# A patch-layout scratch image, the split of a new image one period later, and the blend in the middle of VectorE's period

## The reference, cut to what matters

```
def step(u, _):
    ux, uy, uxx, uxy, uyy = _derivs(u)          # 3x3 and 5x5 stencils, clipped to +-10
    g2 = ux * ux + uy * uy
    denK = jnp.maximum(1.0 + g2, EPS)
    K = jnp.clip((uxx * uyy - uxy * uxy) / (denK * denK + EPS), -5.0, 5.0)
    denH = jnp.sqrt(1.0 + g2 + EPS)
    H = ((1.0 + uy * uy) * uxx - 2.0 * ux * uy * uxy + (1.0 + ux * ux) * uyy) / (2.0 * denH ** 3 + EPS)
    H = jnp.clip(H, -5.0, 5.0)
    u = u + DT * jnp.clip(alpha * K + beta * H, -1.0, 1.0)
    return jnp.pad(u[:, :, 1:-1, 1:-1], ((0, 0), (0, 0), (1, 1), (1, 1)), mode='edge')
mixed = 0.7 * u_after_10_steps + 0.3 * x        # layer 0
out = conv(relu(conv(mixed, w1) + b1), w2) + b2 + mixed   # layer 1
```

## Time and profile before

| | us |
|---|---|
| median of 3 runs (40586.49 to 40609.12) | 40605.43 |
| the profiled execution, its own time | 40599.69 |
| its span in the trace | 40597.9 |
| PE busy | 34779.5 (86%) |
| DVE busy | 34223.0 (84%) |
| ACT busy | 33168.8 (82%) |
| POOL busy | 20444.4 (50%) |

### The profile page before, as it was taken

One profiled execution on the slowest core, in us unless ns is written; L12 is line 12 of the kernel. 1 busy time (PEld: TensorE's weight loads), 2 busy tenths in 40 slices (PEclk: granted clock), 3 DMA queues, 4 the chain that ended last, 5 costly groups with the idle time before them and its releaser, 6 DMA issues. The chain is left out here.

```text
span 40597.9 us, 445411 instructions
## 1 busy us (share of the span) xinstructions
PE 34779.5 (86%) x120896; PEld 22578.0 (56%) x120896; DVE 34223.0 (84%) x31730; ACT 33168.8 (82%) x33722; POOL 20444.4 (50%) x7685
## 2 busy tenths in 40 slices
PE   5888888888888888888888888888888888888999
PEld 3555555555555555555555555555555555554444
DVE  8999999999999999999999999999999999994111
ACT  5888889888888889888888889888888889885333
POOL 3555555555555555555555555555555555551000
PEclk9999999999999999999999999999999999999999
DMA  7555556555555555555555556555555556554333
GB/s 181 79 78 79 79 75 76 77 79 79 79 79 79 79 74 76 77 79 79 78 78 79 79 74 77 77 79 78 79 79 79 78 76 76 77 78 88 99 99 97
DMA packets 2728323, 3335.51 MB, mean 82 GB/s; under 512 B 2236356, under 2 KB 2236484, under 8 KB 2422212
## 3 DMA queue, kind: packets, MB, share of 16 engines
q1 hardware_dynamic: 2727364, 3324.78, 56.8%
HBM read 626.33 MB, written 301.47 MB: 23 GB/s over the span
## 5 line engine op out<-in xcount | busy, mean ns | idle before, releaser
L645 PE MATMUL tame_slot<-tame_split,tame_M 128*128 128x512 f32 x51200 | 15359.2, 422 | 5684.4 <-DVE tame_ux L516 3252.1
L645 PEld LDWEIGHTS tame_slot<-tame_split,tame_M 128*128 128x128 f32 x51200 | 9234.4, 192 | 11664.9 <-DVE tame_cross L516 3060.2
L645 PE MATMUL tame_slot<-tame_halo,tame_M 112*128 112x512 f32 x51200 | 14449.7, 404 | 0.0
L357 POOL TENSOR_TENSOR tame_split<-tame_U,tame_split 128x1024 fp32r<-128x1024 f32 x2560 | 6230.8, 2434 | 12957.1 <-ACT tame_split L392 12957.1
L645 PEld LDWEIGHTS tame_slot<-tame_halo,tame_M 112*128 112x128 f32 x51200 | 9855.4, 192 | 2544.4
L369 POOL TENSOR_TENSOR tame_ux<-tame_ux,tame_cross 128x1024 f32<-128x1024 f32 x2560 | 8063.4, 3150 | 436.3 <-POOL tame_ux L363 436.3
L363 POOL TENSOR_TENSOR tame_ux<-tame_ux,tame_uy 128x1024 f32<-128x1024 f32 x2560 | 6151.2, 2403 | 2695.9 <-DVE tame_uy L516 2695.9
L655 PE MATMUL tame_slot<-tame_uxy,tame_unit 128*128 128x512 f32 x10240 | 4962.0, 607 | 7.2 <-DVE tame_slot L539 7.2
L432 ACT ACTIVATE tame_slope<-tame_slope 128x2048 f32<-128x2048 f32 x2560 | 4894.9, 1912 | 0.0
L427 ACT ACTIVATE tame_slope<-tame_slope 128x1024 f32<-128x1024 f32 x2560 | 2717.5, 1062 | 2153.1 <-issue 2151.1
L558 DVE TENSOR_TENSOR tame_uyy<-tame_slot,tame_slope 128x1024 f32<-128x1024 f32 x2560 | 3135.7, 1225 | 1201.1 <-PE tame_slot L655 1189.8
(11 more groups left out here) (58 smaller groups left out, 36779.3 us busy)
## 6 DMA issues: line engine op xcount, KB each, us to landing
tame_halo<-tame_split SPq DMA_DIRECT2D x2560, 520.0 KB
tame_halo<-tame_split SPq DMA_DIRECT2D x2560, 260.0 KB
tame_halo<-tame_split SPq DMA_DIRECT2D x5120, 65.0 KB
xin<-mixed SPq DMA_DIRECT2D x672, 319.0 KB, 4.3
tame_U<-in_x SPq DMA_DIRECT2D x256, 512.0 KB, 3.7
tame_stage<-in_x SPq DMA_DIRECT2D x128, 1024.0 KB, 8.4
mixed<-tame_stage SPq DMA_DIRECT2D x1024, 128.0 KB, 2.5
out<-res SPq DMA_DIRECT2D x672, 192.0 KB
```

The costliest lines, as they stand in the source:

```text
L357: nc.gpsimd.tensor_tensor(split_rows(c, 1), half_rows(c), split_rows(c, 0).bitcast(F32), ALU.subtract).then_inc(lo_ready, 2)
L645: last = nc.tensor.matmul(ps[name][:, b * BANK:(b + 1) * BANK], M[0:lanes, matrix, :], rows(c, part)[:, b * y:(b + 1) * y, :], start=(n < ...
```

## The change

In layer 0 it does five things.

- `mixed` keeps the patch layout: one partition's 8 KB stay together, and a store is one DMA instead of ten.
- Even and odd columns swap their halves of a patch row (`place`); the partitions that exchange and edge copies touch form the same pattern as before.
- `high` and `low` of a chunk come one period later (k-4 instead of k-3). `scale` moves from the end of ACT's period to behind `copy_ux` of the next one, and `blend` from the start of DVE's period to behind `multiply_first`.
- SP's period is in another order: first `edge_columns` and `edge_rows` of chunk k-2 together, then stage load and half load, then the whole `exchange`, then the store.
- All eight copies of an exchange are issued in one go.

In layer 1 the two side strips of an `xin` row are no longer loaded. DVE makes them (`wrap`, two copies of 63 columns), a row is loaded in pieces of 256 B, and each product is one matmul of 512 columns and four of 256. The loop over 86 units is unrolled.

```
 def place(c):
-    return c // 2 + c % 2 * (PC // 2)
+    return c // 2 + (1 - c % 2) * (PC // 2)
...
             def store(r, i):
-                for to, col, x0, n in ([(PX + k * PX, k, 0, PX) for k in range(PC)]
-                                       + [(1, PC - 1, 0, PX - 1), (PX + PC * PX, 0, 1, PX - 1)]):
-                    sp.dma_start(rows[:, :, to:to + n],
-                                 tile[place(col):P:PC, :, x0:x0 + n]).then_inc(stored[i % 2], 16)
+                image = mixed[bass.ds(r // (C // SLOTS), 1), :, bass.ds(r % (C // SLOTS) * SLOTS + i, 1), :, :]
+                sp.dma_start(image.rearrange("b r o g c -> (b r o) g c"), stage[i % 2][:, :]).then_inc(stored[i % 2], 16)
 
             def period(t, k, kind, r):
+                c = k - 2
+                if exists(kind, c):
+                    edge_columns(t, c)
+                    edge_rows(t, c)
...
-                filling = k % 2 == 0 and kind != "tail" and not (kind == "last" and k == CHUNKS - 2)
-                image, j = (k + 2) % CHUNKS // 2, (k + 2) % 4 // 2
-                if filling:
+                if k % 2 == 0 and kind != "tail" and not (kind == "last" and k == CHUNKS - 2):
                     sp.wait_ge(lo_ready, split_done(t, k - 5))
                     sp.sem_inc(split_whole, 1)
                     if not (kind == "first" and k == 0):
                         sp.wait_ge(product[LAST_FIELD], done(t, k - 1))
-                    exchange(image, j, 0)
-                c = k - 2
-                if exists(kind, c):
-                    edge_columns(t, c)
-                if filling:
-                    exchange(image, j, 1)
-                if exists(kind, c):
-                    edge_rows(t, c)
+                    exchange((k + 2) % CHUNKS // 2, (k + 2) % 4 // 2)
...
-                if exists(kind, k - 3) and goes_on(kind, k - 3):
-                    low(t, k - 3)
+                if exists(kind, k - 4) and goes_on(kind, k - 4):
+                    low(t, k - 4)
...
+                if exists(kind, k - 3) and ends(kind, k - 3):
+                    scale(r, k - 3)
...
-                if exists(kind, k - 3) and goes_on(kind, k - 3):
-                    next_high(t, k - 3, kind, r)
+                if exists(kind, k - 4) and goes_on(kind, k - 4):
+                    next_high(t, k - 4, kind, r)
...
-                if exists(kind, k - 2) and ends(kind, k - 2):
-                    scale(r, k - 2)
...
             def period(t, k, kind, r):
-                if exists(kind, k - 3) and ends(kind, k - 3):
-                    blend(t, k - 3, r)
...
                     multiply_first(t, k)
+                if exists(kind, k - 3) and ends(kind, k - 3):
+                    blend(t, k - 3, r)
...
+            def load(b, u):
+                signal = x_top_in if u == 0 else x_bottom_in if u == UNITS - 1 else x_in[(u - 1) % BUFS]
+                for p0, y, n in rows_of(u):
+                    rows = mixed[bass.ds(b, 1), y % PR:y % PR + n, :, :, y // PR * PX:(y // PR + 1) * PX]
+                    sp.dma_start(source(u)[p0:p0 + n * C, PX:PX + W],
+                                 rows.rearrange("b r c g x -> (b r c) g x")).then_inc(signal, 16)
...
+                nc.vector.tensor_copy(t[:, 1:PX], t[:, HALF:HALF + PX - 1])
+                nc.vector.tensor_copy(t[:, PX + W:PX + W + PX - 1], t[:, PX + HALF + 1:PX + HALF + PX]).then_inc(
+                    x_wrapped, 1)
...
             def product(out_ps, weights, cols, src):
-                for dx in range(K):
-                    last = nc.tensor.matmul(out_ps, weights[:, dx, 0:cols], src[:, dx * PX:dx * PX + W],
-                                            start=(dx == 0), stop=(dx == K - 1))
+                nc.tensor.matmul(out_ps, weights[:, 1, 0:cols], src[:, PX:PX + W], start=True, stop=False)
+                for dx, half, at in ((0, 0, PX + HALF), (0, 1, 0), (2, 0, 2 * PX + HALF), (2, 1, PX)):
+                    last = nc.tensor.matmul(out_ps[:, half * HALF:(half + 1) * HALF], weights[:, dx, 0:cols],
+                                            src[:, at:at + HALF], start=False, stop=(dx == 2 and half == 1))
                 return last
```

More of the change, by code:

```diff
@@ L684, in residual_convolutions @@
 def residual_convolutions(nc, mixed, w1, b1, w2, b2, out):
-    B, H, C, _ = mixed.shape
-    W = PC * PX
+    B, C = out.shape[:2]
+    H, W = PY * PR, PX * PC
     K = 3
@@ L740, in residual_convolutions, with source, count @@
         WEIGHT_DMAS = 2 * NEW * (K + 1)
-        def units(eng, unit):
-            with eng.Fori(0, B) as b:
-                unit(b, 0, b * UNITS + 1, 0, "top", None)
-                with eng.Fori(0, ROUNDS) as i:
-                    for k in range(BUFS):
-                        unit(b, i * BUFS + (k + 1), b * UNITS + i * BUFS + (k + 2), (k + 1) % 2, k, i)
-                unit(b, UNITS - 1, b * UNITS + UNITS, 1, "bottom", None)
+        def source(u):
+            return xtop if u == 0 else xbottom if u == UNITS - 1 else xin[(u - 1) % BUFS]
+        def count(b, u):
+            return b * UNITS + (u + 1)
         @block.sync
@@ L791, in _ @@
[L791 to L800 removed]
+                for u in list(range(BUFS + 1)) + [UNITS - 1]:
+                    load(b, u)
@@ L801, in _ @@
+                for u in range(UNITS):
+                    store(b, u)
+                    if 1 <= u < UNITS - 1 - BUFS:
+                        load(b, u + BUFS)
             for j in range(2):
@@ L826, in hidden @@
                                          ACT.Copy).then_inc(hidden_ready, 1)
-            units(act, hidden)
+            with act.Fori(0, B) as b:
+                for u in range(UNITS):
+                    hidden(b, u)
         @block.vector
@@ new lines, in output @@
+            def output(b, u):
+                pe.wait_ge(hidden_ready, count(b, u) + 2)
+                pe.wait_ge(out_ready, count(b, u))
+                product(po[u % 2][0:NEW_P, :], W2, NEW_P, hid[u % 2]).then_inc(out_product, 1)
+            with pe.Fori(0, B) as b:
+                hidden(b, 0)
+                for u in range(1, UNITS):
+                    hidden(b, u)
+                    if u < UNITS - 1:
+                        output(b, u - 1)
+                output(b, UNITS - 2)
+                output(b, UNITS - 1)
```

162 lines of the change are left out of this document (69 added, 93 removed).

## The result

The changed kernel takes 42,107.4 us (median of 4 runs, 42,084.4 to 42,115.3), the kernel before 40,603.3: ratio 1.037, 95% interval 1.0352 to 1.0388. It is slower by 1,504 us. The profiled execution took 42,115.3 us with a span of 42,113.5, at a mean granted clock of 0.956 (before 0.971).

What follows compares the result with a forecast made beforehand. Layer 0 was taken as a tight ring of DVE and PE, layer 1 as bound by PE. 40,599.7 - 1,724 (image changes) + 3,328 (pairs) + 190 + 16 (layer 1) = 42,410, say 42,400 us; range 41,000 to 44,200.

Steps and rivals of the forecast that it cites:

- the cost per pair: Layer 0's pairs of periods: each grows by 2.6 us (2.1 to 3.1), +3,328 us over 1,280 pairs.
- The first copy of the exchange at +8.32: SP in layer 0: the exchange's first copy issues 8.32 us after DVE's `term_uyy` ends, where it had -1.11 before.
- From the first copy to `ux`, 22.7 us: Layer 0's exchange: 22.7 us from the first copy's issue to PE's `ux` when PE waits for it.
- The excess of 4.2 us: Layer 0: the exchange lets PE begin chunk k+2 at +31.0 instead of +26.8, 4.2 us late.
- The recurrence: Layer 0's stalls: PE late by D makes the next exchange less late by D; D = (4.2 - c)/2.
- The point of decision, 18.5 us: Layer 0's exchange: first issue to last landing must take at most 18.5 us for the exchange to land in time.
- The first rival: Layer 0: the exchange still lands in time and only the image-change gain shows, 39,080 us, faster; chance 0.13.
- The changes of images, -1,724: Layer 0's 31 image changes: stalls go, each costs some 20 us instead of 75.6, gaining 1,724 us (1,100 to 2,190).
- Layer 1, +206: Layer 1: half passes add 190 us (131 to 260), first loads and wraps at starts of batches 16.
- The pitch of 1 MiB: `mixed` patch rows 1 MiB apart may slow a 1 MB store to some 6.4 us, still inside one odd period.
- the second rival: Layer 1 becomes bound by its loads of 256 B pieces, 2,000 us on top, 44,400; chance 0.05.

Runs made afterwards that it cites:

- e2: The kernel before with only the exchange moved, in one go, behind edge columns and rows: 43,545.4 us, ratio 1.0718.
- e3: The changed kernel without the four corner copies of each exchange: 38,834.2 us.
- e4: The changed kernel with three matmuls of 512 columns per layer 1 product, instead of one of 512 and four of 256: 42,113.1 us.
- e5: The changed kernel with the exchange early again, in two parts around the edge columns, and stage loads ahead of it: 39,516.8 us, ratio 0.9734.
- e1: The changed kernel with the exchange back at the front of SP's period, in two parts with the edge columns between: 39,541.9 us, ratio 0.9733.
- e10: Against e5, edge columns and rows go ahead of the exchange where the chunk is about to be blended: 39,683.2 us, ratio 0.9773.
- e12: Against e5, periods about to blend issue large copies, edge columns, edge rows, then corner copies last: 39,621.6 us, ratio 0.9754.
- e11: The changed kernel with the four corner copies issued ahead of the four large copies of the exchange: 44,537.7 us.
- e8: Against e5, the blend at the start of DVE's period and scaling at the end of ACT's, as in the kernel before: 40,499.5 us, ratio 0.9974.

## Why the prediction was right, point by point

Predicted 42,400 us, slower; measured 42,107. The direction, the cause and the cost per pair came out; three terms were mis-sized, and partly cancelled.

- **The first copy of the exchange at +8.32.** Columns to exchange was to take 2.54 + 0.99 = 3.53 us and took 3.44. Right.
- **From the first copy to `ux`, 22.7 us.** Measured 21.97 and 23.16 in the two exchanges shown, mean 22.6. The one late exchange in the trace of before was the right row to take, though it came in two parts.
- **The excess of 4.2 us, shared by two stalls.** The recurrence was right: what one stall delays, the next exchange has in hand. Nothing in it makes the shares equal, and I took them to be. In the double pair shown they came as 3.40 and 0.19 us over the usual 1.29, 3.59 in all. The rest of its 4.63 us, 1.04, lies behind the long stall, at the granted clock of 0.72. I had charged part of a slow clock to each pair (2.6); it comes once in two, and a pair cost 2.37. The term was 3,328 and measured 3,027; e2, which has this edit alone, gave 2,920.
- **The point of decision, 18.5 us.** The first rival needed the exchange to land within it. e3 showed that it would have: without the corners' tail it did, within 14.3 us, and the time fell to 38,834. What speaks against the rival is thus the tail with four packets in flight, not the 1,820 KB.
- **The changes of images, -1,724.** Measured 48.0 us a round, 1,488 in all, where 55.6 was forecast. The stalls of the blends did go (1410.1 to 3.1 us), but PE had longer waits for the exchange than I allowed for (8.21 and 8.27 us at two places of one change):

```profile
1587.43 2.07 PE L631 MATMUL tame_slot<-tame_split,tame_M 128*128 128x512 f32 x4 [8.21 <-DMA tame_halo<-tame_split]
...
1624.60 2.08 PE L631 MATMUL tame_slot<-tame_split,tame_M 128*128 128x512 f32 x4 [8.27 <-DMA tame_halo<-tame_split]
```

- **What the parts gave.** I credited the ten store DMAs, the mid-period blend and the later split together and didn't price them. With the exchange first, the layout gives 330 us, and blend and split give 75.6 - 51.6 = 24 us a round, 744 in all, on the old layout.
- **Layer 1, +206.** The step that failed is "a half pass cannot come faster than" 0.24 us. I took the spacing of layer 0's weight loads for a limit; four matmuls there take 0.95 us as well (1109.38 to 1110.33), so the loads may just follow them. In layer 1 the loads lie 0.21 us apart, and a unit takes 5.17 us (39604.19 to 39609.36), not 5.4. Layer 1 took 16 us longer, and e4, with full passes and the same loads and wraps, none. So the 16 us are what the half passes cost, where 190 were forecast, and the starts of batches, forecast at 16, cost nothing. That 16 stood in both places is chance.
- **The pitch of 1 MiB.** The figure that the Trainium skill gives for 2 MiB (DMA: Bandwidth & Descriptors, Latency and other measured facts) made it an estimated 6.4 us for a store of 1 MB. The list of transfers (KB each, median us to landing) shows 6.5, though here only every eighth partition lies 1 MiB from the one before:

```profile
mixed<-tame_stage SPq DMA_DIRECT2D x128, 1024.0 KB, 6.5
xin<-mixed SPq DMA_DIRECT2D x344, 256.0 KB, 4.6
```

It was hidden as forecast, and so were the loads of 256 B pieces; the second rival fell.

The versions that came out best are e5, 39,517 us, and e1, 39,542, which their ratios (0.9734, 0.9733) don't tell apart: 2.7% below the kernel before, and e5 6.2% below the changed one. e1 keeps every edit but the exchange's new place, and e5 also issues the stage loads ahead of it.

## What to carry to other kernels

A change that bundles several moves can hide a good one behind a bad one. Price the step that is issued in every period first: 2.4 us in each of 1,280 pairs outweighed 48 us in each of 31 changes. For a large group of copies, count the packets on the engine that holds the most, not the bytes: four small copies of four partitions made an exchange half as long again (22.2 us to the end of its last packet, 14.3 without them). When two consumers wait behind one queue, reordering it moves the wait from one to the other (e5, e10, e12); only less traffic, or a better spread, removes it.

## What the runs showed of the hardware that I had not expected

**A stall that lasts in alternation.** The pattern long, short, long, short held through the middle bodies, in the changed kernel and in e2, and most of the short ones are no stall at all. With the corners first (e11) each pair stalls, one by 2.89 and one by 6.27 us.

**VectorE waits for GpSimd.** The mean blend rose from 1225 to 1691 ns. The timelines of GpSimd and of VectorE show two kinds:

```profile
1508.53 3.14 POOL L355 TENSOR_TENSOR tame_ux<-tame_ux,tame_cross 128x1024 f32<-128x1024 f32 x1 [0.17 <-POOL tame_ux L349]
```

```profile
1510.50 2.26 DVE L502 SCALAR_TENSOR_TENSOR tame_stage<-tame_U,tame_stage 128x1024 f32<-128x1024 f32 x1
...
1527.88 1.22 DVE L502 SCALAR_TENSOR_TENSOR tame_stage<-tame_U,tame_stage 128x1024 f32<-128x1024 f32 x1
```

The blend that begins at 1510.50 ends 1.09 us after GpSimd's addition does (1511.67). The one at 1527.88, with GpSimd done, takes 1.22. The Trainium skill has the rule (SBUF — State Buffer, two separate sides): a VectorE operation with two operands in SBUF and a GpSimd operation that reads SBUF share a pair of ports, which whichever comes first holds to its end. The trace agrees. At its old place, the period's start, the blend never met GpSimd (mean 1225 in e8 too); in the middle it does, for 256 x 0.47 = 119 us of VectorE in all. It does so when it needn't wait: e5 has it at the same place, but behind a wait for rows, and its mean is 1247.
